# Subtracting the row maximum of the scores in PSUM by matmuls, and another order for the last tiles' routing

## The chip, the cores and the metric

The kernel runs on one core of a Trainium2 chip. The metric is the time of one execution on the device in microseconds (us); the kernel before took 1230.69 us, the median of 3 runs (1223.26 to 1238.8). The engines are TensorE (PE; its weight loads are PEld), VectorE (DVE), ScalarE (ACT), GpSimd (POOL) and SyncE (SP), which only issues transfers here. Each runs its own list of instructions in order, and they wait for one another through semaphores.

## The reference

The layer is a gated cross attention followed by a gated mixture of experts, 32 batches of 256 rows, 256 wide; the context has 77 rows a batch, 16 heads of width 16.

```python
x = x + tanh(g_xattn) * xattn(layernorm(x), ctx, ctx, mask, Wq, bq, Wk, bk, Wv, bv, Wfc, bfc)
x = x + tanh(g_ffn) * ffn(layernorm(x), gate_kernel, w0, w1, wo)

# xattn
energy = einsum('bhqd,bhkd->bhqk', Q, K) / 4
energy = where(mask == 0, -1e10, energy)
attention = softmax(energy, axis=-1)
x = einsum('bhqk,bhkd->bhqd', attention, V) @ Wfc.T + bfc      # heads merged

# ffn: 8 experts, each row goes to the 2 with the largest gate logits
top_k_weights, top_k_indices = top_k(x @ gate_kernel, 2)
weights = softmax(top_k_weights)
output = sum over the 2 experts of weight * ((silu(x @ w0[e]) * (x @ w1[e])) @ wo[e])
```

## The kernel before, in words

The 8192 rows are 64 tiles of 128 query rows, two tiles to a batch. The first part goes through the 32 batches: layer norm, projections, attention, residual, second layer norm, gate, choice of two experts, and a scatter of each row (256 values, its number and its weight) to a buffer in device memory, `routed_rows`, sorted by expert. The second part goes through 135 tiles of that buffer, one expert a tile, and adds the result to the output by an indirect transfer. Between them, DVE computes tables that say which tile belongs to which expert. Expert weights are split in a high and a low part during the first part, stored as `split_weights`, and fetched again.

Every engine has its own hand-written list: one function `batch(b, u, n)` per engine, called for batches 0 to 3 and 30, 31 as straight code and in a loop for the others. The order of the calls there is the order of the work. In it `i` is the batch's first tile, and the work for several tiles is in flight: while tile `i` attends, the scores of `i + 1` are in PSUM, and the gate and routing of tiles `i - 1` to `i - 4` are under way.

The path of a tile's scores: PE writes the mask and the scores of all 16 heads (4 heads in each of 4 PSUM banks, 308 columns in each, 1232 in all) into `psS`, which is single-buffered (`scores`, L1454 and L1460). DVE takes the maximum of each head (`s_largest`, L1075), then subtracts it and writes the result to `prob` in SBUF (`s_shift`, L1079). ACT takes the exponential in place (`exp_scores`, L711). PE transposes `prob` in three groups through `psT` (`prob_T`, L1475), ACT copies each to `probT` (L707), and PE multiplies with the values and a column of ones (`attend`, L1489, 32-column tiles). DVE normalises (L1087, L1090), PE transposes and projects (`o_T` L1499, `project` L1507), DVE adds the residual (L1100). The second norm's output is transposed by `n2_T` (L1517), the gate is L1525, the ranks within an expert are L1530 and L1531. The low part of the next batch's queries is `q_low` (L1033), awaited by the value projection (L1433).

At the end of the first part each engine has straight code for the last tiles. DVE's `route` chooses experts and places rows; POOL numbers rows, computes weights (`weigh`) and scatters (L568, two transfers a tile); SP stores the last split weight piece (`store_piece`, L418), the last output tile (L431), and writes padding rows at the ends of the experts' regions (`pad_experts`, L378), ACT pads the other half. POOL loads the first routed rows (L620) only when the tables, all output tiles, all pads and all scatters are done.

Of the kernel before, what the change touches and what calls it, by code (L numbers as in the profile page):

```python
# [15 lines left out]
P = 128  # L16
# [6 lines left out]
def flamingo_gated_layer(nc, x, ctx_in, mask, g_xattn, g_ffn, Wq, bq, Wk, bk, Wv, bv, Wfc, bfc,  # L23
# [57 lines left out]
    with ExitStack() as ctx, ExitStack() as attention:  # L81
# [85 lines left out]
        mx = sb("mx", [P, 2, H])  # L167
# [68 lines left out]
        psY = psG[:, D:2 * D]  # L236
        assert H * VW + DC * K2 <= 512 and E == 8
# [19 lines left out]

        s_ps, s_max, s_sub, p_done = sem("s_ps"), sem("s_max"), sem("s_sub"), sem("p_done")
# [127 lines left out]
        def _(sp):  # L386
# [69 lines left out]
            batches(sp, batch)  # L456
            store_piece(NQ - 1)
            store_x1(NT - 1, 1)

            pad_experts(sp, range(0, E, 2))  # L460
# [28 lines left out]
        def _(gp):  # L489
# [114 lines left out]
            rstd_2(NT - 1)  # L604
            for i in range(NT - 4, NT):
                number_rows(i, i % 4)
            weigh(B - 2, 0)
            scatter(NT - 4, 0, B - 2)
            scatter(NT - 3, 1, B - 2)
            weigh(B - 1, 1)  # L610
# [50 lines left out]
        def _(act):  # L661
# [47 lines left out]
            def exp_scores(i, t):  # L709
                act.wait_ge(s_sub, i + 1)  # L710
                act.activation(prob[:, t, 0:HK], prob[:, t, 0:HK], ACT.Exp, scale=scale).then_inc(p_done, 1)  # L711
# [152 lines left out]
            o_evac(NT - 1)  # L864
            norm_2(NT - 2, 0, 2, LOOPS - 1)
            n2_evac(NT - 2)
            exp_gap(NT - 3, 1, B - 2)
            gated_evac(NT - 2)
            copy_row(NT - 2, 2)
            norm_2(NT - 1, 1, 3, LOOPS - 1)  # L870
            n2_evac(NT - 1)
# [88 lines left out]
        def _(dve):  # L960
# [34 lines left out]
            dve.memset(prob[:, :, HK:CH * P], 0.0).then_inc(valid_done, 1)  # L995
            dve.wait_ge(valid_done, 17)
# [3 lines left out]
            dve.tensor_copy(pick_key[:].rearrange("p (o k) -> p o k", o=3), ident[0:K2, 0:K2].rearrange("p (o k) -> p o k", o=1).to_broadcast([K2, 3, K2])).then_inc(valid_done, 1)  # L1000
            dve.wait_ge(mask_in[0], 16)
# [71 lines left out]
            def s_largest(i, t):  # L1073
                dve.wait_ge(s_ps, RG * (i + 1))
                dve.tensor_reduce(mx[:, t].rearrange("p (n h) -> p n h", n=RG), S_ALL, AX_X, ALU.max).then_inc(s_max, 1)  # L1075

            def s_shift(i, t):
                dve.wait_ge(s_max, i + 1)
                dve.tensor_tensor(prob[:, t, 0:HK].rearrange("p (n h k) -> p n h k", n=RG, k=K2), S_ALL,  # L1079
                                  mx[:, t].rearrange("p (n h o) -> p n h o", n=RG, o=1).to_broadcast([P, RG, HB, K2]),  # L1080
                                  ALU.subtract).then_inc(s_sub, 1)
# [84 lines left out]
            s_shift(0, 0)  # L1166
# [4 lines left out]
            def batch(b, u, n):  # L1171
# [22 lines left out]
                s_shift(i + 1, 1)  # L1194
# [45 lines left out]
                if more:  # L1240
                    s_shift(i + 2, 0)
# [29 lines left out]
            stats_2(NT - 2, 0, 1)  # L1271
            residual_1(NT - 1, 1, 1, B - 1)
            for part in range(2):
                stats_2(NT - 1, 1, part)
            for i in range(NT - 3, NT):
                route(i)
# [106 lines left out]
        def _(pe):  # L1383
# [62 lines left out]
            def scores(i, u, t, b):  # L1446
# [3 lines left out]
                if known(i, 1):  # L1450
                    pe.wait_ge(s_sub, i)
# [4 lines left out]
                for q_part, k_part in PARTS:  # L1456
                    for c in range(DC):
                        for j in range(RG):
# [43 lines left out]
            def project(i):  # L1502
                pe.wait_ge(oT_sb, DC * (i + 1))
                if known(i, 1):
                    pe.wait_ge(n2T_sb, i)
# [4 lines left out]
            def n2_T(i, u4):  # L1510
                pe.wait_ge(xn2_done, i + 1)
                if below(i, NT - 1):
# [36 lines left out]
            flatten_values(0)  # L1549
            ctx_T(1, 1, 0)  # L1550
            pe.wait_ge(gate_in, 16)
            keys(1)
            x_T(1)
# [3 lines left out]
            def batch(b, u, n):  # L1557
# [39 lines left out]
                if known(i + 1, 2):  # L1597
                    n2_T(i - 1, (u4 - 1) % 4)
                attend(i + 1, u, b, 1)
                attend(i + 1, u, b, 2)  # L1600
# [168 lines left out]
```

## Time and profile before

| what | value |
|---|---|
| median of 3 runs | 1230.69 us (1223.26 to 1238.8) |
| the profiled execution | 1230.18 us |
| its span, first to last instruction | 1228.6 us |
| mean granted TensorE clock | 0.962 of full |
| PE busy, of the span | 1123.8 us (91%) |
| DVE busy | 956.0 us (78%) |
| ACT busy | 702.7 us (57%) |
| POOL busy | 729.3 us (59%) |
| chain that ended last: PE, DVE, issue, DMA | 78%, 8%, 6%, 4% |
| maxima of the scores (L1075), 64 times | 91.8 us busy, 1435 ns each |
| subtraction (L1079), 64 times | 91.5 us busy, 1430 ns each |

The first part ends at about 560 us of the span, the second begins at about 586 us. The shares are averages over both parts, so what the change touches must be read inside the first part and at the passage between them.

### The profile page before, as it was taken

The numbers are of one execution on the slowest core, as the hardware profiler recorded it, in microseconds if no ns is written. First come the engines' busy times: TensorE is split into PE (matmuls) and PEld (weight loads), VectorE is DVE, ScalarE is ACT, GpSimd is POOL, SyncE is SP. The second block draws the span as 40 slices with busy tenths as digits, with TensorE's granted clock in tenths as the row PEclk, the third lists the DMA queues.
The fourth block names the chain that finished last, engine by engine and source line by source line (L and its number), as shares of the span: only waits on it lengthen the run. The fifth ranks groups of instructions, "written<-read, shape, count | busy, mean of one in ns | idle before, by whom it ended". The sixth has DMA issues, their size and how long they took to land.

```text
span 1228.6 us, 46148 instructions
## 1 busy us (share of the span) xinstructions
PE 1123.8 (91%) x14850; PEld 922.4 (75%) x14851; DVE 956.0 (78%) x2702; ACT 702.7 (57%) x1652; POOL 729.3 (59%) x1134
## 2 busy tenths in 40 slices
PE   3999999999999999960899999999879999999994
PEld 2787888888888888740788888888758888888883
DVE  4798999999999999845344688888668888888882
ACT  2787888888888888840343344444334444444441
POOL 3367888888888888744244455555435555555552
PEclk9999999999999999975899999999989999999997
DMA  5144444444444444464688576767888666666672
GB/s 163 34 136 150 152 151 151 151 150 146 144 148 146 146 146 151 142 222 151 197 227 215 114 124 119 120 119 119 156 126 129 120 120 120 119 121 120 120 117 26
DMA packets 193909, 169.74 MB, mean 138 GB/s; under 512 B 130996, under 2 KB 174548, under 8 KB 191668
## 3 DMA queue, kind: packets, MB, share of 16 engines
q1 hardware_dynamic: 158592, 112.54, 34.4%
q0 software_dynamic: 32064, 52.46, 22.3%
q10 hardware_dynamic: 3188, 3.89, 1.4%
q8 instruction: 38, 0.62, 0.2%
q14 instruction: 27, 0.22, 0.1%
HBM read 68.95 MB, written 70.27 MB: 113 GB/s over the span
## 4 chain that ended last, share of the span: by engine, by line
PE 78%; DVE 8%; issue 6%; DMA 4%; ACT 1%; POOL 1%; ACTq 1%; DVEq 0%; POOLq 0%; SPq 0%
PE banks L1658 29%; PE psB L1679 9%; PE psB L1489 5%; PE psT L1475 5%; PE psB L1682 5%; PE psG L1507 5%; PE psA L1426 3%; PE banks L1460 3%; PE psA L1433 3%; PE psG L1637 2%; DMA hT<-hs 2%; PE psA L1443 2%; DVE mx L1075 2%; PE psG L1499 2%; DVE prob L1079 1%
## 5 line engine op out<-in xcount | busy, mean ns | idle before, releaser
L1658 PE MATMUL banks<-w_all,etT 128*128 x1620 | 431.5, 403 | 12.6 <-DVE etT L1345 11.5
L633 POOL DMA_INDIRECT out_dram<-ey,eid x135 | 216.7, 1605 | 218.1 <-PE psG L1637 106.8
L1658 PEld LDWEIGHTS banks<-w_all,etT 128*128 128x128 f32 x1620 | 288.1, 190 | 62.3 <-DVE etT L1345 12.4
L909 ACT ACTIVATE ey<-psB,ewt 128x256 f32<-128x256 f32 x135 | 64.2, 476 | 191.0 <-PE psB L1682 190.8
L620 POOL DMA_DIRECT2D et<-routed_rows x135 | 101.3, 750 | 115.1 <-issue 114.9
L568 POOL DMA_INDIRECT routed_rows<-rows,slot x128 | 126.5, 988 | 44.9 <-issue 33.5
L1679 PE MATMUL psB<-w_all,hgT 128*128 x540 | 147.2, 394 | 4.7 <-DVE ey L1355 3.9
L881 ACT CAST etT<-psG 128x256 fp32r<-128x256 f32 x135 | 50.6, 375 | 151.6 <-PE psG L1637 148.9
L707 ACT COPY probT<-psT 128x512 f32<-128x512 f32 (+1 forms) x192 | 98.9, 515 | 48.9 <-PE psT L1475 46.5
L1679 PEld LDWEIGHTS psB<-w_all,hgT 128*128 128x128 f32 x540 | 100.8, 189 | 29.2 <-issue 5.9
L1475 PE MATMUL psT<-ident,prob 128*128 128x128 f32 x640 | 104.9, 279 | 7.0 <-ACT gated L733 4.2
L1355 DVE SCALAR_TENSOR_TENSOR ey<-psB,ewt,ey 128x256 f32<-128x256 f32 x135 | 65.2, 483 | 50.5 <-ACT ey L909 49.9
L890 ACT ACTIVATE hs<-banks 128x512 f32<-128x512 f32 x135 | 80.9, 600 | 35.8 <-PE psT L1668 32.5
L1341 DVE COPY hT<-hT 128x1024 uint16<-128x1024 uint16 x113 | 84.5, 748 | 18.2 <-DMA hT<-hs 16.9
L1345 DVE TENSOR_TENSOR etT<-psG,etT 128x256 fp32r<-128x256 f32 x135 | 57.1, 423 | 49.3 <-ACT etT L881 48.6
L1075 DVE TENSOR_REDUCE mx<-banks 128x16 f32<-128x1232 f32 x64 | 91.8, 1435 | 3.0 <-PE banks L1460 3.0
L1322 DVE TENSOR_TENSOR hs<-banks,hs 128x512 f32<-128x512 f32 x135 | 92.3, 683 | 1.8 <-PE banks L1658 1.8
L1682 PEld LDWEIGHTS psB<-w_all,hgT 128*128 128x128 f32 x540 | 83.3, 191 | 11.4
L1079 DVE TENSOR_TENSOR prob<-banks,mx 128x1232 f32<-128x1232 f32 x64 | 91.5, 1430 | 0.1
L1475 PEld LDWEIGHTS psT<-ident,prob 128*128 128x128 f32 x640 | 75.7, 143 | 20.4 <-issue 9.4
L1334 DVE COPY hs<-hs 128x1024 uint16<-128x1024 uint16 x113 | 79.4, 702 | 12.4
L1489 PE MATMUL psB<-vbd,probT 128*32 128x51 f32 x5120 | 87.6, 212 | 0.0
(177 smaller groups left out, 2335.2 us busy)
## 6 DMA issues: line engine op xcount, KB each, us to landing
split_weights<-w_part SPq DMA_DIRECT2D x16, 1536.0 KB, 6.2
w_all<-split_weights SPq DMA_DIRECT2D x28, 768.0 KB, 4.5
et<-routed_rows POOLq DMA_DIRECT2D x135, 129.0 KB
xb<-in_x_dram SPq DMA_DIRECT2D x32, 256.0 KB, 3.1
w_raw<-in_L_ffn_w_kernel_dram SPq DMA_DIRECT2D x32, 256.0 KB
out_dram<-x SPq DMA_DIRECT2D x64, 128.0 KB
w_raw<-in_L_ffn_wo_kernel_dram SPq DMA_DIRECT2D x16, 256.0 KB
cb<-in_ctx_dram SPq DMA_DIRECT2D x32, 77.0 KB
```

The lines of the kernel that those rows point to most:

```text
L568: gp.indirect_dma_start(out=routed, out_offset=bass.IndirectOffsetOnAxis(ap=slot[:, u4, k:k + 1], axis=0), in_=rows[:, u4, k, :], in_offse ...
L620: gp.dma_start(et[:, u % 2], routed[bass.ds(r * P, P), :]).then_inc(et_in[u % 2], 16)
L633: gp.indirect_dma_start(out=out, out_offset=bass.IndirectOffsetOnAxis(ap=eid[:, u % 8:u % 8 + 1], axis=0), in_=ey[:, u % 4, :], in_offset= ...
L707: act.copy(probT[:, c0:c1].rearrange("p c q -> p (c q)"), psT[:, 0:(c1 - c0) * P]).then_inc(t_sb, 1)
L1075: dve.tensor_reduce(mx[:, t].rearrange("p (n h) -> p n h", n=RG), S_ALL, AX_X, ALU.max).then_inc(s_max, 1)
L1079: dve.tensor_tensor(prob[:, t, 0:HK].rearrange("p (n h k) -> p n h k", n=RG, k=K2), S_ALL, mx[:, t].rearrange("p (n h o) -> p n h o", n=RG ...
L1322: dve.tensor_tensor(hs[:], banks4[:, 2 + u % 2], hs[:], ALU.mult).then_inc(hg_done, 1)
L1475: m = pe.transpose(psT[:, (c - c0) * P:(c - c0 + 1) * P], prob[:, t, c * P:(c + 1) * P], ident[:])
L1489: m = pe.matmul(psB[r0:r0 + ROWS, h * VW:(h + 3) * VW], probT[:, c, r0:r0 + ROWS], vbd[:, u, c].rearrange("p h d -> p (h d)"), start=(c == ...
L1658: m = pe.matmul(banks4[:, bank], etT[:, u % 2, a, c], weight(e, c, w, n), start=(j == 0), stop=(j == len(steps) - 1))
L1679: pe.matmul(psB[:, 0:2 * D], hgT[:, u % 2, 0, c], weight_pair(e, c), start=(c == 0), stop=False, skip_group_check=True)
L1682: m = pe.matmul(psB[:, 0:D], hgT[:, u % 2, 1, c], weight(e, c // 2, 0, 2, c % 2 * D, D), start=False, stop=(c == FC - 1), skip_group_check ...
```

## The change

In the attention, DVE still takes the maximum of each head, but writes the 16 values of a query row to 16 of 128 columns of a tile `mx`, four at the head of each group of 32 columns. PE multiplies this tile with the identity, which gives its transpose in unused columns of the first score bank (`max_T`). DVE copies the transpose to SBUF (`max_evac`), and PE multiplies it with a constant matrix that has -1 where a head's row meets its 77 columns, accumulating into the scores in PSUM (`shift`, four matmuls of 32 rows, one for each bank). ACT's exponential reads the four banks and writes `prob`. The whole-tile subtraction on DVE is gone; the next tile's scores wait for the exponential instead of the subtraction.

At the end of the first part: PE projects the last tile before it transposes the second-last tile's norm; DVE routes tile NT-3 before the last residual; ACT and POOL take some steps in another order, POOL scatters two tiles before it numbers the last two; SP writes its pads before it stores the last weight piece.

```diff
@@ -164,7 +164,9 @@
-        mx = sb("mx", [P, 2, H])
+        mx = sb("mx", [P, P])
+        mxT = sb("mxT", [P, P], F32R)
+        minus_head = sb("minus_head", [P, HB, K2], F32R)
...
+        psM = psS[:, 0, HB * K2:HB * K2 + P]
@@ -454,10 +458,9 @@
             batches(sp, batch)
+            store_x1(NT - 1, 1)
+            pad_experts(sp, range(0, E, 2))
             store_piece(NQ - 1)
-            store_x1(NT - 1, 1)
-
-            pad_experts(sp, range(0, E, 2))
@@ -601,12 +604,14 @@
             rstd_2(NT - 2)
-            rstd_2(NT - 1)
-            for i in range(NT - 4, NT):
+            for i in range(NT - 4, NT - 2):
                 number_rows(i, i % 4)
             weigh(B - 2, 0)
+            rstd_2(NT - 1)
             scatter(NT - 4, 0, B - 2)
             scatter(NT - 3, 1, B - 2)
+            for i in range(NT - 2, NT):
+                number_rows(i, i % 4)
             weigh(B - 1, 1)
@@ -707,8 +712,10 @@
             def exp_scores(i, t):
-                act.wait_ge(s_sub, i + 1)
-                act.activation(prob[:, t, 0:HK], prob[:, t, 0:HK], ACT.Exp, scale=scale).then_inc(p_done, 1)
+                act.wait_ge(s_sub, RG * (i + 1))
+                if known(i, 2):
+                    act.wait_ge(t_ps, 3 * (i - 1))
+                act.activation(prob[:, t, 0:HK].rearrange("p (n q) -> p n q", n=RG), psS[:, 0:RG, 0:HB * K2], ACT.Exp, scale=scale).then_inc(p_done, 1)
...
             o_evac(NT - 1)
+            exp_gap(NT - 3, 1, B - 2)
             norm_2(NT - 2, 0, 2, LOOPS - 1)
             n2_evac(NT - 2)
-            exp_gap(NT - 3, 1, B - 2)
-            gated_evac(NT - 2)
             copy_row(NT - 2, 2)
             norm_2(NT - 1, 1, 3, LOOPS - 1)
+            gated_evac(NT - 2)
             n2_evac(NT - 1)
@@ -993,11 +1000,17 @@
+            for j in range(RG):
+                r0 = j * ROWS
+                dve.tensor_scalar(minus_head[r0:r0 + ROWS], ident[r0:r0 + ROWS, r0:r0 + HB].rearrange("p (h o) -> p h o", o=1).to_broadcast([ROWS, HB, K2]),
+                                  -1.0, None, ALU.mult).then_inc(head_rows, 1)
...
             def s_largest(i, t):
                 dve.wait_ge(s_ps, RG * (i + 1))
-                dve.tensor_reduce(mx[:, t].rearrange("p (n h) -> p n h", n=RG), S_ALL, AX_X, ALU.max).then_inc(s_max, 1)
-
-            def s_shift(i, t):
-                dve.wait_ge(s_max, i + 1)
-                dve.tensor_tensor(prob[:, t, 0:HK].rearrange("p (n h k) -> p n h k", n=RG, k=K2), S_ALL,
-                                  mx[:, t].rearrange("p (n h o) -> p n h o", n=RG, o=1).to_broadcast([P, RG, HB, K2]),
-                                  ALU.subtract).then_inc(s_sub, 1)
+                if known(i, 1):
+                    dve.wait_ge(mT_ps, i)
+                dve.tensor_reduce(mx[:].rearrange("p (n s) -> p n s", n=RG)[:, :, 0:HB], S_ALL, AX_X, ALU.max).then_inc(s_max, 1)
+
+            def max_evac(i):
+                dve.wait_ge(mT_ps, i + 1)
+                if known(i, 1):
+                    dve.wait_ge(s_sub, RG * i)
+                dve.tensor_copy(mxT[:], psM).then_inc(mT_sb, 1)
...
             stats_2(NT - 2, 0, 1)
+            route(NT - 3)
             residual_1(NT - 1, 1, 1, B - 1)
             for part in range(2):
                 stats_2(NT - 1, 1, part)
-            for i in range(NT - 3, NT):
-                route(i)
+            route(NT - 2)
+            route(NT - 1)
@@ -1448,7 +1464,7 @@
                 if known(i, 1):
-                    pe.wait_ge(s_sub, i)
+                    pe.wait_ge(p_done, i)
...
+            def max_T(i):
+                pe.wait_ge(s_max, i + 1)
+                pe.matmul(psM, mx[:], ident[:], start=False, stop=True, skip_group_check=True).then_inc(mT_ps, 1)
+
+            def shift(i):
+
+                pe.wait_ge(mT_sb, i + 1)
+                for j in range(RG):
+                    r0 = j * ROWS
+                    pe.matmul(psS[:, j, 0:HB * K2], mxT[r0:r0 + ROWS], minus_head[r0:r0 + ROWS].rearrange("p h k -> p (h k)"),
+                              start=False, stop=True, skip_group_check=True).then_inc(s_sub, 1)
...
                 attend(i, u, b, 0)
+                max_T(i + 1)
                 if known(i, 2):
                     n2_T(i - 2, (u4 - 2) % 4)
                 attend(i, u, b, 1)
                 attend(i, u, b, 2)
+                shift(i + 1)
                 if known(i, 1):
                     project(i - 1)
...
             o_T(NT - 1)
+            project(NT - 1)
             n2_T(NT - 2, 2)
-            project(NT - 1)
```

In the calls of DVE's list `s_shift(i, t)` is replaced by `max_evac(i)` at the same place. The orders of instructions below show where this puts the new ones. A name such as `banks<-ident,mx` gives the tile written and those read; `banks` is the score banks, `psT`, `psB`, `psG` and `psA` are the other PSUM tiles.

PE, second half of a batch in the loop, before:

```order
L1489 MATMUL psB<-vbd,probT 32x51 x16
L1438 REGISTER_ALU
L1443 MATMUL psA<-vparts,pick_key 128x48 x30
L1471 REGISTER_ALU
L1475 MATMUL psT<-ident,prob 128x128 x2
L1513 REGISTER_ALU
L1517 MATMUL psG<-ident,rows 128x128 x2
L1489 MATMUL psB<-vbd,probT 32x51 x16
L1480 REGISTER_ALU
L1489 MATMUL psB<-vbd,probT 32x51 x8
L1507 MATMUL psG<-wfcT,onT 128x256 x2
```

and in the changed kernel:

```order
L1545 MATMUL psG<-ident,rows 128x128 x2
L1483 REGISTER_ALU
L1484 MATMUL banks<-ident,mx 128x128
L1517 MATMUL psB<-vbd,probT 32x51 x16
L1508 REGISTER_ALU
L1517 MATMUL psB<-vbd,probT 32x51 x8
L1491 MATMUL banks<-minus_head,mxT 128x308 x4
L1535 MATMUL psG<-wfcT,onT 128x256 x2
```

The maximum's matmul stands between the transposes of the norm (now L1545) and the rest of attending (now L1517), the four shifts between attending and the projection (now L1535).

SP, from the pads to the fetches of the expert weights, in the changed kernel (before, the store of `split_weights` and a store of `out_dram` stood ahead of the pads):

```order
L381 TENSOR_LOAD base_i
L381 ISA x2
L382 ISA
L382 DMA routed_rows<-pad_rows 128x258
L422 DMA split_weights<-w_part 128x3072
L428 DMA w_all<-split_weights 128x1536 x20
```

The rows shown are the last of four pads, the store of the last piece and what follows.

POOL, the last tiles, in the changed kernel:

```order
L554 COPY rows<-token_id 128x2 x2
L560 TENSOR_SCALAR wsum<-egap 128x2
L562 TENSOR_TENSOR wrec<-wsum,neg_one 128x2
L564 TENSOR_TENSOR rows<-wrec,tanhg 128x2
L566 TENSOR_TENSOR rows<-rows,egap 128x2
L543 TENSOR_SCALAR ve<-mv 128x1
L544 TENSOR_SCALAR neg<-mv 128x1
L548 TENSOR_TENSOR rs<-ve,half_neg 128x1
L550 TENSOR_TENSOR shift<-neg,rs 128x1
L571 DMA routed_rows<-rows,slot 67456x258 x4
L554 COPY rows<-token_id 128x2 x2
```

Before, both norms (the rows from `ve` to `shift`) and four copies of row numbers stood ahead of the first weights. Now the weights of tiles 60 and 61 come ahead of the last tile's norm, and their four scatters ahead of the last two tiles' numbers.

## Rows read from the trace of the kernel before

**Rows 1.** Stretches: us, busy time per engine (instructions), granted clock, DMA share, GB/s

```profile
77.50:470.00 392.50, 385.04 (x9111) 315.57 (x9109) 363.94 (x1237) 343.78 (x856) 314.81 (x657) 1.00 0.44 145
```

**Rows 2.** Order of time, PE: start, duration, what, idle before

```profile
118.36 0.81 PE L1426 MATMUL psA<-xnT,wqT 128*128 128x256 f32 x3
...
306.53 1.89 PE L1426 MATMUL psA<-xnT,wqT 128*128 128x256 f32 x8
...
319.50 0.63 PE L1475 MATMUL psT<-ident,prob 128*128 128x128 f32 x4 [0.23 <-ACT gated L733]
...
322.09 1.89 PE L1426 MATMUL psA<-xnT,wqT 128*128 128x256 f32 x8
...
494.69 0.38 PE L1426 MATMUL psA<-xnT,wqT 128*128 128x256 f32 x1
```

**Rows 3.** Waits of PE's weight loads, 77.5 to 505 us: total, times, longest

```profile
PEld psA L1433 <- DVE qT L1033: 1.9, 11, 0.2
```

**Rows 4.** The chain that ended last, in order of time: start, duration, what

```profile
309.14 0.37 PE psG L1517 x2
309.51 0.69 PE psB L1489 x48
...
313.18 0.24 PE banks L1454 x4
...
314.42 0.44 PE psT L1475 x4
...
316.48 0.22 PE psG L1517 x2
...
317.38 1.07 PE psG L1507 x4
318.64 0.48 DVE x L1100
```

**Rows 5.** Groups by line and form, 200 to 472 us: busy us, mean ns, idle before

```profile
L1079 DVE TENSOR_TENSOR prob<-banks,mx 128x1232 f32<-128x1232 f32 x35 | 50.0, 1429 | 0.0
L711 ACT ACTIVATE prob<-prob 128x1232 f32<-128x1232 f32 x35 | 43.2, 1234 | 0.0
L707 ACT COPY probT<-psT 128x512 f32<-128x512 f32 x70 | 41.1, 587 | 9.5 <-PE psT L1475 8.0
...
L1046 DVE SCALAR_TENSOR_TENSOR kT<-psB,bias,valid 128x77 f32<-128x77 f32 x34 | 8.6, 294 | 1.7 <-issue 1.2
```

**Rows 6.** Order of time, 540 to 586 us; the last row is from the page's DMA issues

```profile
548.22 2.05 PE L1507 MATMUL psG<-wfcT,onT 128*128 128x256 f32 x4 [0.55 <-ACT xn2T L721]
550.31 0.48 DVE L1100 SCALAR_TENSOR_TENSOR x<-psG,tanhg,xg 128x256 f32<-128x256 f32 x1 [6.80 <-PE psG L1507]
557.08 1.05 POOL L568 DMA_INDIRECT routed_rows<-rows,slot  x1 [0.82 <-POOL rows L563]
568.44 0.23 DVE L1307 CAST tblk_i<-tblk 128x135 int32<-128x135 f32 x1
569.32 0.96 POOL L568 DMA_INDIRECT routed_rows<-rows,slot  x1 [0.30 <-issue]
570.31 2.49 POOL L574 TENSOR_TENSOR w_part<-w_raw,w_part 128x512 fp32r<-128x512 f32 x2
572.82 0.34 SPq L418 DMA_DIRECT2D split_weights<-w_part  x1
575.24 4.59 SPq L378 DMA_DIRECT2D routed_rows<-pad_rows  x4
583.18 0.61 POOL L620 DMA_DIRECT2D et<-routed_rows  x1 [10.38 <-issue]
585.67 0.66 PE L1637 MATMUL psG<-ident,et 128*128 128x128 f32 x2 [26.69 <-DMA et<-routed_rows]
...
split_weights<-w_part SPq DMA_DIRECT2D x16, 1536.0 KB, 6.2
```

**Rows 7.** Order of time, PE, at the start of the kernel

```profile
30.90 1.25 PE L1409 MATMUL psB<-ctxT,wkT 128*32 128x77 f32 x32 [2.89 <-ACT ctxT L684]
```

More of the change, by code:

```diff
@@ L256, in flamingo_gated_layer @@
         v_nat, v_part, v_rest = sem("v_nat"), sem("v_part"), sem("v_rest")
+        mT_ps, mT_sb, head_rows = sem("mT_ps"), sem("mT_sb"), sem("head_rows")
         s_ps, s_max, s_sub, p_done = sem("s_ps"), sem("s_max"), sem("s_sub"), sem("p_done")
@@ L456, in _ @@
             batches(sp, batch)
-            store_piece(NQ - 1)
             store_x1(NT - 1, 1)
             pad_experts(sp, range(0, E, 2))
+            store_piece(NQ - 1)
             sp.wait_ge(pad_out, 16 * (1 + E + SPARE))
@@ L995, in _ @@
             dve.memset(prob[:, :, HK:CH * P], 0.0).then_inc(valid_done, 1)
+            dve.memset(mx[:], 0.0).then_inc(head_rows, 1)
             dve.wait_ge(valid_done, 17)
@@ L1000, in _ @@
             dve.tensor_copy(pick_key[:].rearrange("p (o k) -> p o k", o=3), ident[0:K2, 0:K2].rearrange("p (o k) -> p o k", o=1).to_broadcast([K2, 3, K2])).then_inc(valid_done, 1)
+            for j in range(RG):
+                r0 = j * ROWS
+                dve.tensor_scalar(minus_head[r0:r0 + ROWS], ident[r0:r0 + ROWS, r0:r0 + HB].rearrange("p (h o) -> p h o", o=1).to_broadcast([ROWS, HB, K2]),
+                                  -1.0, None, ALU.mult).then_inc(head_rows, 1)
+            dve.wait_ge(head_rows, 1 + RG)
             dve.wait_ge(mask_in[0], 16)
@@ L1165, in _ @@
             s_largest(0, 0)
-            s_shift(0, 0)
+            max_evac(0)
             v_evac(0, 0)
@@ L1193, in batch @@
                     k_low(b + 1)
-                s_shift(i + 1, 1)
+                max_evac(i + 1)
                 if known(i, 3):
@@ L1240, in batch @@
                 if more:
-                    s_shift(i + 2, 0)
+                    max_evac(i + 2)
                 o_norm(i + 1, 0)
@@ L1504, in project @@
                 if known(i, 1):
-                    pe.wait_ge(n2T_sb, i)
+                    pe.wait_ge(n2T_sb, i if below(i, NT - 1) else i - 1)
                 for c in range(DC):
@@ L1511, in n2_T @@
                 pe.wait_ge(xn2_done, i + 1)
-                if below(i, NT - 1):
+                if below(i, NT - 2):
                     pe.wait_ge(oT_sb, DC * (i + 2))
@@ L1549, in _ @@
             flatten_values(0)
+            max_T(0)
             ctx_T(1, 1, 0)
@@ L1552, in _ @@
             keys(1)
+            shift(0)
             x_T(1)
@@ L1598, in batch @@
                     n2_T(i - 1, (u4 - 1) % 4)
+                if more:
+                    max_T(i + 2)
                 attend(i + 1, u, b, 1)
                 attend(i + 1, u, b, 2)
+                if more:
+                    shift(i + 2)
                 if known(i + 1, 1):
```

## The prediction

> **What bounds the kernel now.** I read the stretches first, then the tensor engine's order of time, then the chain of waits, and last the single durations. One stretch covers the steady attention loop: there the matmul row of TensorE (PE below) is busy for 385.04 of 392.5 us, VectorE (DVE) for 363.94, ScalarE (ACT) for 343.78, at full granted clock [rows 1]. The reader should see two engines near full, so the next question is which one sets the pace. The start of the query projection marks a batch (two tiles of 128 query rows). From 306.53 to 322.09 a batch takes 15.56 us; from 118.36 to 494.69 there are 24, 15.68 us each on average, so that the other of each pair takes about 15.80 [rows 2]. PE has one visible stall in the 15.56 us batch, 0.23 us before the transposes of the probabilities, which wait for ACT [rows 2]; the longer batch has 0.2 us more, before the value projection, waiting for DVE's low part of the queries [rows 3]. Without stalls PE needs 15.56 - 0.23 = 15.33 us. So PE is the bound, and at most 15.68 - 15.33 = 0.35 us a batch can come back by relieving DVE.
>
> At the junction between attention and experts PE stands still for 26.69 us until the first routed rows are there [rows 6].
>
> **DVE, per tile.** Removed: the subtraction over 1232 columns, 1.43 us. Added: a copy of 128 PSUM columns. Two rows bracket it, 0.29 us for 77 columns and 0.48 us for 256; by their slope (0.19/179 per column) 128 columns are an estimated 0.34 us [rows 5, 6]. DVE loses 1.09 us of work a tile, 2.2 a batch. But it isn't the bound. It must also wait inside its queue: the new copy stands where the subtraction was and waits for the transposed maximum, which PE issues only after the first part of attending. Behind it stand the low part of the queries, the normalisation and the residual. In the batch that begins at 306.53 PE reached that place 2.6 us later, at 309.14 [rows 4]. With the added matmul and 0.34 us of copy DVE goes on at about 310.0, some 1 us later than now; the queries' low part is then ready at about 311.8, and PE, itself later by both new groups, asks for it at about 312.1. I cost this wait at nothing; its cover is the 0.3 us just named.
>
> **ACT, per tile.** The exponential takes 1.23 us from SBUF. From PSUM, ACT copied 512 columns in 0.59 us, so 1232 columns are at most 1.41 us by that rate, and 1.23 if the source doesn't matter [rows 5]. I take 1.23: ACT has 1.9 us a batch free. Its chain (PE's shift, the exponential, the gate's copy, then the next transposes) takes some 1.7 us, while PE has the output projection (1.1), gate, rank and keys or values to do in between, about 2.0 to 2.3. So the exponential's new place in the chain costs nothing, and the 0.23 us stall goes, since PE comes 0.5 us later. The scores' new wait for the exponential costs nothing either: in PE's order the transposes of the same tile's probabilities stand ahead of it and need the same event.
>
> **PE, per tile: the term that counts.** Added: one fp32 matmul of the maximum with the identity, 128 columns, and four row-tiled matmuls of 308 columns. The trace has no such fp32 matmul. The nearest rows are the transposes, four of 128 columns in 0.44 us. A full fp32 matmul appears as two records, so twice 0.11 = 0.22 us. The upper bound is a pair of transposes right behind column-tiled work, 0.37 [rows 4]. In the first half of a batch the new one stands ahead of just such a pair and takes over its change of mode, in the second behind one. So I take 0.25. For the four shifts the nearest row is the mask's group, also four matmuls of 308 columns: 0.24 us, a change of mode included [rows 4]. It is bf16 where the shift is a 32-bit type, so I take 0.28, with 0.24 and 0.40 as ends. Sum 0.53 us a tile, from 0.46 to 0.77.
>
> A rule speaks against the change here. Attending with 32-column tiles and then projecting at full width already costs a change of mode (a pair takes 0.37 us behind attending and 0.22 behind a transpose, 0.15 between them [rows 4]); the shift puts a third mode in between. The Trainium skill, "TensorEngine Tiling (Array Packing)", Key Properties, says that a change of tiling mode drains the engine. Both agree. If the mask's 0.24 did not contain that drain, a tile would cost 0.15 more and the sum below 9.3 us more.
>
> 62 tiles lie in the stretch that PE bounds: 62 x 0.53 = +32.9 us. Recovered: 0.35 us a batch for 29 batches, -10.2 us. Net +22.7. A new batch is then 15.33 + 1.06 = 16.4 us.
>
> **The start.** The builds of the -1 matrix (four of 308 columns) go into DVE's idle time before the first weights: free. For the first tile PE does the maximum ahead of the second context's transposes and keys. Those keys ran at 30.90 us, before the first maximum was ready [rows 7]; they now come about 1.3 us later, and the first exponential with them. Against that, DVE's chain gets shorter over the next two tiles. I take +1, with -2 and +3 as ends.
>
> **The junction.** Three edits, read from the same rows [rows 6]:
> 1. Projection of the last tile ahead of the second-last tile's normalised transposes. It started at 548.22 though its own input was there at about 544.3: PE stood before the transposes ahead of it, for ACT. It now starts at about 544.4; the last residual, DVE at 550.31, comes about 4 us sooner, and with it the last routing and the tables, finished at 568.7 and now at about 564.6.
> 2. Scatters. GpSimd (POOL) issued all eight from 557.08 to 570.28, about 1.3 us each. Four can now go at about 550 to 555, the other four when the last slots are ready, 558 to 563.3. Then the two low parts (2.49 us): POOL is free at about 565.8 instead of 572.8.
> 3. SyncE's queue. The pads were issued from 575.24 to 579.83, behind the store of the last weight piece, which waited for POOL until 572.82. Only then, at 583.18, were the first routed rows asked for. The pads' own condition was met at 560. Ahead of the store they end by about 562.5, and no longer count.
> So the load of the first rows is issued at about 566 instead of 583.18: 17 us. Late next is the store: its 1.5 MB takes 6.2 us and now runs beside that load, which took 2.4 us alone. If the load lands with the store, 4 us are lost. I take -15.5, ends -17 and -11.
>
> **Sum.** The profiled execution took 1230.18 us (span 1228.6), 0.5 us under the median of the runs, 1230.69. 1230.2 + 22.7 + 1 - 15.5 = 1238.4. Forecast **1238 us**: slower by 0.6%, which is no difference at the 2% (24.6 us) that I take as the least a measurement of this kernel can tell, its runs lying 1223 to 1239.
>
> **Rivals.**
> - *Tight waits and changes of mode (slower).* A tile costs PE the upper 0.77 us, and in the second half of each batch only part of attending (0.69 us) covers the way from the maximum over DVE's copy to the shift: a handoff to DVE of 0.2 (PE's projection ends at 318.45, DVE begins at 318.64 [rows 4]), the copy 0.34 and a handoff back of the same 0.2 fill it entirely. If they exceed it by 0.3, 31 batches cost 9 us more. 1230.2 + 47.7 + 9 - 10.2 + 1 - 15.5 = 1262. It is over 2% from 0.8 us a tile in all. For it: each handoff has a cost that PE can't hide. Against it: the only groups with such shapes take 0.22 to 0.37 and 0.24. Chance 0.13.
> - *The junction gives little.* The store delays the load of rows, or the scatters still end last because the weights of the last pair wait for the last gap: -5 instead of -15.5, 1249. For it: the store's transfer and the rows' use the same 16 engines. Chance 0.15.
> - *The new matmuls hide (faster).* Were DVE the true bound, PE's added work would fall into its slack: 1230.2 - 10.2 + 1 - 15.5 = 1205.5. Against it: PE's pieces stand end to end in the chain in both halves. Chance 0.05.
> - *DVE becomes later.* The wait for the maximum holds up the queries' low part by more than the 0.3 us of cover, and the 0.35 us a batch are not recovered: 1238.4 + 10.2 = 1249. Chance 0.12.
> - Forecast as worked out: 0.55.
>
> **Range.** The ends of the forecast's own terms are 1238.4 - 4.3 (0.46 a tile) - 1.5 - 3 = 1230 and, with one upper end, 1253. Reaching halfway to the faster rival and over both rivals at 1249 gives **1219 to 1256**. Slower by over 2% (above 1254.8): the first rival and a tail of others, 0.16. Faster by over 2% (below 1206): 0.05. Within: 0.79.
>
> **What would show it.** In the new profile: batches of 16.4 us between query projections; the new matmul of the maximum at about 0.25 us and the group of four at about 0.28 in the chain; no stall of PE for the gate's copy or the queries' low part; DVE idle around 1 us a batch ahead of the new copy; the first load of routed rows issued about 17 us sooner after the end of attention. The prediction is wrong if the batch is at or below 15.7 us (the matmuls hide), above 16.8 (waits or mode changes), or if pads, scatters or the store still stand in the chain before that load.

## The result, and the profile after

The changed kernel takes 1244.28 us (median of 9 runs, 1241.91 to 1250.84), the kernel before 1229.32 in the runs beside it (9 runs, 1222.44 to 1240.23): ratio 1.0118, 95% interval 1.0079 to 1.0158. It is 1.2% slower, in the range of 1219 to 1256; the forecast was 1238. The effect itself was about twice the forecast one: 15.0 us between the medians, where 0.6% (7.7 us) was forecast.

From the page of the changed kernel: the busy time of its engines, and the share of each in the chain of work that ended last.

```profile
PE 1155.6 (93%) x15234; PEld 946.7 (76%) x15235; DVE 890.1 (72%) x2707; ACT 712.7 (57%) x1652; POOL 728.9 (59%) x1134
...
PE 91%; DMA 3%; issue 2%; DVE 2%; ACT 1%; POOL 1%; ACTq 1%; POOLq 0%; SPq 0%; DVEq 0%
```

DVE lost 66 us of work and its share of the chain fell from 8% to 2%. PE gained 32 us of busy time, and the kernel got longer with PE and not shorter with DVE. The steady loop shows it better. The stretch of [rows 1] in the changed kernel (busy time per engine in the same order):

```profile
77.50:470.00 392.50, 390.43 (x8926) 318.23 (x8925) 296.13 (x1177) 332.96 (x810) 297.67 (x621) 1.00 0.42 138
```

PE is busy for 99.5% of it, DVE for 75% (before 98% and 93%). The starts of the query projection, as in [rows 2], in the order of time of PE:

```profile
56.08 0.38 PE L1442 MATMUL psA<-xnT,wqT 128*128 128x256 f32 x1
...
308.29 0.38 PE L1442 MATMUL psA<-xnT,wqT 128*128 128x256 f32 x1
...
324.88 0.38 PE L1442 MATMUL psA<-xnT,wqT 128*128 128x256 f32 x1
...
540.61 0.38 PE L1442 MATMUL psA<-xnT,wqT 128*128 128x256 f32 x1
```

Every steady batch takes 16.59 us, where they alternated between 15.56 and 15.8: +0.91 on the average of 15.68. The new groups stand in the chain, first half of a batch and then second half:

```profile
310.91 0.42 PE banks L1484 x2
311.32 0.22 PE psG L1545 x2
311.54 0.69 PE psB L1517 x48
312.23 0.34 PE banks L1491 x3
312.57 1.06 PE psG L1535 x4
...
318.81 0.22 PE psG L1545 x2
319.03 0.22 PE banks L1484 x2
319.25 0.69 PE psB L1517 x48
319.94 0.34 PE banks L1491 x3
```

The maximum's matmul takes 0.42 us behind attending, but relieves the transposes after it of 0.15 (0.22 us, and 0.37 in [rows 4]), net 0.27; behind transposes it takes 0.22. The four shifts take 0.34. The other pieces keep their length to within 0.06 us, except the transposes of x, which take 0.60 in this chain and 0.44 in that of E5, where they come up again. DVE waits for the maximum, PE does not wait for DVE's copy (waits from 77.5 to 505 us, total, times, longest):

```profile
DVE mxT L1096 <- PE banks L1484: 53.6, 51, 1.9
```

The junction in the order of time, the rows that answer to [rows 6]; SPq is SyncE's queue of transfers:

```profile
580.61 5.87 SPq L428 DMA_DIRECT2D w_all<-split_weights  x2
586.52 0.45 SPq L435 DMA_DIRECT2D out_dram<-x  x1
588.51 4.37 SPq L382 DMA_DIRECT2D routed_rows<-pad_rows  x4
593.61 0.34 SPq L422 DMA_DIRECT2D split_weights<-w_part  x1
...
591.10 2.48 POOL L577 TENSOR_TENSOR w_part<-w_raw,w_part 128x512 fp32r<-128x512 f32 x2
599.05 0.61 POOL L625 DMA_DIRECT2D et<-routed_rows  x1 [5.46 <-issue]
```

From these marks the 14.1 us between the two spans divide as follows. The marks of before are 52.01 and 510.25 for the second and the last query projection, and 583.18 for the first load of routed rows [rows 6].

| stretch | before | after | difference | forecast |
|---|---|---|---|---|
| start to the second query projection | 52.0 | 56.1 | +4.1 | +1 |
| to the last one, 30 batches | 458.2 | 484.5 | +26.3 | +22.7 (whole stretch) |
| to the first load of routed rows (junction) | 72.9 | 58.4 | -14.5 | -15.5 |
| to the end of the span | 645.4 | 643.7 | -1.8 | 0 |

One batch of the 30 is not steady, the one in which the straight code gives way to the loop: 19.57 us before and 20.43 in the changed kernel. In the changed kernel PE stops in it for 2.07 us, without a wait that the profile shows, and then runs at the lower of its two clocks (granted clock 0.50, which is 1.2 GHz) for some 3 us. Order of time, and the stretch from 120 to 123 us in the columns of [rows 1]:

```profile
119.38 0.47 PE L1491 MATMUL banks<-minus_head,mxT 32*128 32x308 f32 x3 [2.07 <-issue]
119.77 2.07 PE L1535 MATMUL psG<-wfcT,onT 128*128 128x256 f32 x4
```

```profile
120.00:123.00 3.00, 3.00 (x54) 2.43 (x54) 0.95 (x2) 1.83 (x4) 0.60 (x1) 0.50 0.23 80
```

The projection of four matmuls takes 2.07 us there and 1.13 in the steady loop. The kernel before has the same thing (a stop of 2.60 us, granted clock 0.50 from 112 to 115), so it cancels between these two. Between the kernels below it does not.

### The profile page after: what moved, and what is told of

Its sections match the earlier page's. It is cut to its first block, busy times and chain, and to the rows that moved or that the text cites. A ratio compares the mean times of both kernels' runs of the same rounds, so it can differ in the third digit from the quotient of the medians.

```text
span 1242.7 us, 47084 instructions
## 1 busy us (share of the span) xinstructions
PE 1155.6 (93%) x15234; PEld 946.7 (76%) x15235; DVE 890.1 (72%) x2707; ACT 712.7 (57%) x1652; POOL 728.9 (59%) x1134
## 4 chain that ended last, share of the span: by engine, by line
PE 91%; DMA 3%; issue 2%; DVE 2%; ACT 1%; POOL 1%; ACTq 1%; POOLq 0%; SPq 0%; DVEq 0%
PE banks L1694 30%; PE psB L1715 10%; PE psT L1503 6%; PE psB L1517 6%; PE psG L1535 5%; PE psB L1718 5%; PE psA L1442 5%; PE banks L1476 3%; PE psG L1673 2%; PE psA L1449 2%; PE psA L1459 2%; PE psG L1527 2%; PE banks L1491 2%; PE banks L1484 2%; PE psB L1425 2%
## 5 line engine op out<-in xcount | busy, mean ns | idle before, releaser
L1715 PE MATMUL psB<-w_all,hgT 128*128 x540 | 147.1, 394 | 4.8 <-DVE ey L1371 3.9
L1517 PE MATMUL psB<-vbd,probT 128*32 128x51 f32 x5120 | 85.5, 211 | 2.0 <-issue 2.0
L1718 PE MATMUL psB<-w_all,hgT 128*128 x540 | 85.8, 282 | 0.0
```

The lines of the kernel that those rows point to most:

```text
L1517: m = pe.matmul(psB[r0:r0 + ROWS, h * VW:(h + 3) * VW], probT[:, c, r0:r0 + ROWS], vbd[:, u, c].rearrange("p h d -> p (h d)"), start=(c == ...
L1715: pe.matmul(psB[:, 0:2 * D], hgT[:, u % 2, 0, c], weight_pair(e, c), start=(c == 0), stop=False, skip_group_check=True)
L1718: m = pe.matmul(psB[:, 0:D], hgT[:, u % 2, 1, c], weight(e, c // 2, 0, 2, c % 2 * D, D), start=False, stop=(c == FC - 1), skip_group_check ...
```

## The experiments

Each kernel's median stands beside the kernel before on the same chip, as a ratio. Stage times are from each kernel's profiled execution. Steady batches repeat to 0.02 us. The stretches before and after them, and the batch at the entry of the loop, differ by some us even between kernels that share PE's order, so they count for less.

**E1 and E2: the two halves of the change by themselves.** E1 keeps the attention part and undoes the end; E2 keeps the end and lets DVE subtract.

Three of the end's edits, E1 against the changed kernel:

```diff
+            store_piece(NQ - 1)
             store_x1(NT - 1, 1)
...
-            store_piece(NQ - 1)
...
-            route(NT - 3)
...
-            route(NT - 2)
-            route(NT - 1)
+            for i in range(NT - 3, NT):
+                route(i)
...
+            n2_T(NT - 2, 2)
             project(NT - 1)
-            n2_T(NT - 2, 2)
```

E2 makes the opposite edits to the kernel before, and so keeps DVE's subtraction.

> The change's attention part alone; the end of the first part is in the old order. Theory A (PE's own added work sets the batch, the new order of the end is a separate gain): batches of 16.59 us as in the changed kernel, the first routed rows asked for about 73 us after the last query projection as before the change, total about 1229 + 0.91 x 29 + 4 = 1260 us. Rival (the parts lean on one another, the end gains only because DVE is freed): the end is short here too, total about 1245.

> The kernel before with the new order of the end alone. Theory A: batches 15.56 and 15.8 us, the first routed rows asked for about 58 us after the last query projection, total about 1229 - 16 = 1213 us. Rival: the end stays near 73 us because DVE still subtracts there, total 1225 to 1229.

E1 took 1255.99 us, ratio 1.0238 (1.0168 to 1.0307); E2 took 1213.07 us, ratio 0.9861 (0.98 to 0.9921). Batches of 16.59 us in E1; 15.55 and 15.8 in E2. E1, the last query projection and the first load of rows:

```profile
536.82 0.38 PE L1440 MATMUL psA<-xnT,wqT 128*128 128x256 f32 x1
...
610.10 0.61 POOL L624 DMA_DIRECT2D et<-routed_rows  x1 [10.55 <-issue]
```

E2, the same two marks:

```profile
507.82 0.38 PE L1428 MATMUL psA<-xnT,wqT 128*128 128x256 f32 x1
...
567.24 0.61 POOL L621 DMA_DIRECT2D et<-routed_rows  x1 [8.19 <-issue]
```

That is 73.3 us in E1 (old end, DVE relieved) and 59.4 in E2 (new end, DVE subtracting), against 72.9 and 58.4 in the kernels before and after. The gain at the end does not need the relieved DVE. The change is two changes of opposite sign: the attention part costs 2.4%, the end gives 1.4%.

**E3: no maximum and no shift.** It leaves out the maximum, its transpose, the copy and the shift, and gives masked keys -60 instead of -1e10.

```diff
-MASKED = -1e10
+MASKED = -60.0
...
-                max_T(i + 1)
...
-                shift(i + 1)
...
-                act.wait_ge(s_sub, RG * (i + 1))
+                act.wait_ge(s_ps, RG * (i + 1))
```

> The changed kernel without the maximum, its transpose and the shift: the exponential reads the scores as they are, and masked keys get -60 where they had -1e10. Theory A: PE's batch falls by its two groups, 2 x (0.22 + 0.34) and what they cost their neighbours, to 15.4 to 15.5 us, total about 1207. Rival (another engine would be the bound at once, for instance DVE's residual and value copies ahead of PE's transposes of x): 15.7 or more, total 1215 or more.

1207.19 us, ratio 0.9807 (0.974 to 0.9873); batch 15.53 us:

```profile
252.85 0.60 PE L1434 MATMUL psA<-xnT,wqT 128*128 128x256 f32 x2
...
268.39 0.60 PE L1434 MATMUL psA<-xnT,wqT 128*128 128x256 f32 x2
```

Here DVE does neither maximum nor subtraction, 2.86 us a tile less than before, and PE does exactly the work of before. The forecast's bound was 0.35 us back by relieving DVE, a batch of 15.33. E3 gained 0.15 on 15.68. PE's stall for ACT's copy of the gate is still there, though no maximum is waited for:

```profile
250.27 0.63 PE L1495 MATMUL psT<-ident,prob 128*128 128x128 f32 x4 [0.20 <-ACT gated L740]
```

So that stall was not DVE's. It lies in ACT's queue, where two activations of the next norm (1.1 us) stand ahead of the exponential and the copy, without a gap (order of time):

```profile
247.84 1.10 ACT L696 ACTIVATE xn<-xb,shift,rs 128x256 f32<-128x256 f32 x2
248.84 1.19 ACT L718 ACTIVATE prob<-banks 128x1232 f32<-128x1232 f32 x1
249.92 0.18 ACT L740 COPY gated<-psT 128x24 f32<-128x24 f32 x1
```

**E4: the same operations in bf16.** Waits and order are those of the changed kernel. The subtracted value needs no precision, since the same rounded maximum leaves all keys of a head and cancels in the softmax.

```diff
-        mx = sb("mx", [P, P])
-        mxT = sb("mxT", [P, P], F32R)
-        minus_head = sb("minus_head", [P, HB, K2], F32R)
+        mx = sb("mx", [P, P], BF16)
+        mxT = sb("mxT", [P, P], BF16)
+        ident16 = sb("ident16", [P, P], BF16)
+        minus_head = sb("minus_head", [P, HB, K2], BF16)
...
-                pe.matmul(psM, mx[:], ident[:],
+                pe.matmul(psM, mx[:], ident16[:],
```

> The changed kernel with the maximum, its transpose and the -1 matrix in bf16; all waits, handoffs and the instruction order stay. Theory A (work sets the batch): the maximum's matmul falls from 0.22 to about 0.08 us, the shift from 0.34 to between 0.24 (like the mask's group) and 0.34; batch 16.1 to 16.35 us, total about 1232 to 1239. Rival (handoffs from PE over DVE back to PE set it): batch 16.5 to 16.6, total 1243. If the shift stays at 0.34, its excess over the mask's group is the change of tiling mode, not the type.

1223.67 us, ratio 0.9971 (0.9945 to 0.9997). Batch 15.97 us, 0.62 less. In the chain, the second half of one batch and the first half of the next:

```profile
257.36 0.06 PE banks L1486
257.41 0.69 PE psB L1519 x48
258.10 0.24 PE banks L1493 x4
...
265.56 0.16 PE banks L1486
265.73 0.23 PE psG L1547 x2
265.95 0.69 PE psB L1519 x48
266.64 0.24 PE banks L1493 x4
```

The maximum falls from 0.42 and 0.22 to 0.16 and 0.06 us, the shift from 0.34 to 0.24: 0.26 + 0.16 + 2 x 0.10 = 0.62, all of the batch's gain. Theory A holds: every handoff stayed as it was, and the batch fell by the work alone. The maximum's matmul in bf16 was expected at 0.08 us. It took that or less behind transposes and twice that behind attending, but the net saving was larger than expected, so the batch (16.1 to 16.35 expected) and the total (1232 to 1239 expected) both came out below their bounds. E4 also settles why the shift was longer than the mask's group: it was the 32-bit type. In bf16 it equals the mask's 0.24 [rows 4], in spite of its place between 32-column tiles and full width. With the new end, however, even the bf16 form (0.9971 of the kernel before) is slower than DVE's subtraction (E2, 0.9861).

**E5: what PE waits for before the transposes of x, and the start.** In the changed kernel the gate's stall was gone, but the weight load for the transposes of x came 0.18 us late; DVE's copy of the values ends just ahead of it, at 306.00 (order of time):

```profile
304.95 0.48 DVE L1115 SCALAR_TENSOR_TENSOR x<-psG,tanhg,xg 128x256 f32<-128x256 f32 x1 [0.69 <-PE psG L1535]
305.35 0.65 DVE L1078 TENSOR_TENSOR vbd<-psA,head_of 128x480 f32<-128x480 f32 x1
306.12 0.42 PEld L1435 LDWEIGHTS psA<-ident,xn 128*128 128x128 f32 x4 [0.18 <-issue]
```

```diff
+                if more:
+                    v_evac(b + 1, 1 - u)
                 if known(i + 1, 1):
                     residual_1(i, u, 0, b)
-                if more:
-                    v_evac(b + 1, 1 - u)
...
+            ctx_T(1, 1, 0)
             max_T(0)
-            ctx_T(1, 1, 0)
+            shift(0)
             pe.wait_ge(gate_in, 16)
             keys(1)
-            shift(0)
             x_T(1)
```

> The changed kernel with two orders altered: DVE copies the next batch's values ahead of the residual, and at the start PE does the second context's transposes ahead of the first maximum, and the first shift ahead of the keys. Theory A (the 0.18 us that PE waits before the transposes of x comes from DVE's copy of the values standing behind the residual): that wait goes and the batch is 16.4 us; at the start the delay of 4 us against the kernel before falls to 2 to 3. Total about 1237 us. Rival (the transposes of x wait for something else, as ACT's norm): batch 16.59, total 1242.

1239.71 us, ratio 1.0108 (1.0073 to 1.0144). The batch is 16.42 us (252.07 to 268.49), and the second query projection starts at 52.54 instead of 56.08:

```profile
52.54 0.38 PE L1442 MATMUL psA<-xnT,wqT 128*128 128x256 f32 x1
...
252.07 0.60 PE L1442 MATMUL psA<-xnT,wqT 128*128 128x256 f32 x2
...
268.49 0.38 PE L1442 MATMUL psA<-xnT,wqT 128*128 128x256 f32 x1
```

The wait was DVE's residual ahead of the values' copy: 0.17 us a batch. E5 also corrects the base of the forecast. Less the new groups (0.49 + 0.68) its batch is 15.25 and not 15.33, so 0.08 more comes back than the 0.23 of the stall's row. The projection behind the shift is a part of that: 1.06 us in the first half of a batch, and 1.10 in E3 without the shift.

The start's order is worth some 2 to 3 us: four kernels with the changed order reach this mark at 54.7 to 56.1 us, four with the altered one at 51.3 to 53.7. The five kernels with DVE's subtraction reach it at 52.0 to 55.1. Kernels of one order thus differ by up to 3 us, and the size is uncertain. The total of 1239.7 lies between the two expectations, 1237 and 1242; the batch decides for the first.

**E6: what still ends last at the junction.** SyncE fetches weight pieces 2 and 3 behind the pads instead of in the last batch.

```diff
+                fetch = early and u == 0
-                if early:
+                if fetch:
...
-            for q in range(EARLY, RING):
+            for q in range(DC, RING):
```

> The changed kernel with the fetches of weight pieces 2 and 3 moved on SyncE from the last batch to behind the pads. Theory A (after the change the pads still end last at the junction, because SyncE's queue holds the fetches): the first routed rows are asked for about 53 us after the last query projection instead of 58.4, total about 1239. Rival (the scatters or the tables end last anyway): 57 to 58 us, total 1244.

1255.22 us, ratio 1.0224 (1.0165 to 1.0282): a miss in the total, though the junction did what was expected. The marks are 539.81 and:

```profile
594.32 0.61 POOL L626 DMA_DIRECT2D et<-routed_rows  x1 [1.76 <-issue]
```

54.5 us, 3.9 less. Without the fetches the pads go out at 582.66, 42.9 us after the last query projection instead of 47.9. But four more transfers (4.3 to 6.7 us each) now stand on SyncE's queue ahead of the first transposes of the expert part, which the queue issues at tile 20. The end of the fetches on SyncE, and PE's first long stall in the expert part:

```profile
702.50 11.71 SPq L428 DMA_DIRECT2D w_all<-split_weights  x3
714.35 13.56 SPq L483 DMA_TRANSPOSE hT<-hs  x4
...
720.75 1.22 PE L1695 MATMUL banks<-w_all,etT 128*128 x2 [10.50 <-DVE etT L1362]
```

In the changed kernel the queue is free at 691.8, 92.7 us after the first load of rows, and no stall stands at this place; here it is 120 us after it. From the first load to the end E6 takes 658.1 us, 14.4 more than the changed kernel, and this stall is 10.5 of them. The 3.9 us won at the junction do not cover it.

**E7 and E8: the end of E6 with DVE's subtraction, and with bf16.** Both also copy the values ahead of the residual; E8 has the altered start of E5 as well, which is not shown. The lines stand against E2 for E7, and against E4 for E8.

```diff
-                if early:
+                fetch = early and u == 0
+                if fetch:
...
-            for q in range(EARLY, RING):
+            for q in range(DC, RING):
...
+                if more:
+                    v_evac(b + 1, 1 - u)
                 if known(i + 1, 1):
                     residual_1(i, u, 0, b)
-                if more:
-                    v_evac(b + 1, 1 - u)
```

> The kernel before (DVE subtracts) with the new order of the end, the values copied ahead of the residual, and the fetches behind the pads. Theory A: batches as before the change or 0.05 us shorter, the end 5 us shorter than in the kernel with the new end alone, total about 1207 us.

> The maximum by matmuls in bf16 with the values' copy ahead, the altered start and the fetches behind the pads. Theory A: batch 15.97 - 0.18 = 15.8 us, junction about 53 us, total about 1223.7 - 5 - 2 - 5 = 1212 us. Rival: one of the three doesn't add up with the others, 1218 or more.

E7: 1220.46 us, ratio 0.9964 (0.9931 to 0.9998). E8: 1225.94 us, ratio 0.9995 (0.9968 to 1.0022). The batches are as expected (15.54 and 15.83; 15.80), so the values' copy gives E7 nothing, where PE doesn't wait for it. The junctions take 52.4 and 56.6 us. Both miss their totals by 13 to 14 us (1207 and 1212 were expected). PE's stall at the first transposes, with the queue free 115 and 114 us after the first load, is a part of it: 4.59 us in E7 and 7.25 in E8. In E7's profiled execution (1215.77, its fastest run) the stretch after the first load is 7.8 us longer than E2's, which takes back the 7.0 gained at the junction; why the median lies 4.7 above that run is open. E8's junction stayed 3.6 us over the 53 that were expected, and its last stretch is 11.9 longer than E4's, more than the stall. I estimated from the 10.5 us at 120 that the queue may be busy until about 109 us without a stall; E7 and E8 give 110 and 107 in the same way.

**E9, E10, E12: only piece 3 behind the pads**, two transfers instead of four: DVE's subtraction without the values' order (E9), bf16 (E10) and fp32 (E12) with all the orders above.

```diff
-            for q in range(EARLY, RING):
+            for q in range(EARLY - 1, RING):
```

> The kernel before with the new order of the end, and only weight piece 3 (two transfers) moved behind the pads. Theory A (in e6 the junction got shorter, but four more transfers on SyncE's queue held up the first transposes of the expert part; the queue may end up to about 109 us after the first rows are asked for): junction 53 to 54.5 us, queue ends at about 107 us, no stall of PE over 2 us near tile 22, total about 1213 - 4 = 1209 us. Rival (the stall comes from something else that moving any fetch causes): a stall of some us stays, total 1213 or more.

> The maximum by matmuls in bf16, the values' copy ahead, the altered start, and only weight piece 3 behind the pads. Theory A: as e8 without its 7 us stall, total about 1217 us. Rival: 1224 or more.

> The changed kernel with the values' copy ahead, the altered start and only weight piece 3 behind the pads; the maximum stays fp32. Theory A: batch 16.42 us, junction about 55 us, total about 1239.7 - 4 = 1235 us, so 18 us more than the same kernel in bf16 (30 batches of 0.62).

| kernel | median us | ratio (95%) | batch | junction |
|---|---|---|---|---|
| E9 | 1216.83 | 0.9904 (0.9875 to 0.9932) | 15.55, 15.8 | 54.3 |
| E10 | 1215.36 | 0.9899 (0.9857 to 0.994) | 15.80 | 55.7 |
| E12 | 1238.15 | 1.008 (1.004 to 1.012) | 16.43 | 57.4 |

The stall at the first transposes is gone in all three; in E9 the queue is free 105 us after the first load. E10 (1217 expected) is 22.8 us faster than E12 (1235 expected), of which 30 x 0.62 = 18.6 are the type. E9 was expected at 1209 and is no faster than E2. Its profiled execution reached the second query projection 2.1 us later than E2's (55.14 against 53.08), its batch at the entry of the loop took 20.29 us where E2's took 15.86, and its last stretch was 2.7 us longer, against 5.1 gained at the junction. E2 and E9 differ in SyncE's list alone. In E9 PE stopped for 3.32 us in the entry batch and ran at a granted clock of 0.50 from 117 to 119 us, and E2 shows neither. Each has one profiled execution, so whether such a step belongs to the kernel or to the run isn't shown, and whether E9's shorter junction is worth anything stays open. The best kernel with matmuls (E10, 0.9899) is no faster than the two with DVE's subtraction (E2 0.9861, E9 0.9904), so no run here shows a gain from moving the subtraction.

**E11: the 0.23 us stall, by ACT's order.** E2 with the exponential ahead of the next norm.

```diff
-                if more2:
-                    norm_1(b + 2, u)
                 if more:
                     exp_scores(i + 2, 0)
+                if more2:
+                    norm_1(b + 2, u)
```

> The kernel before with the new order of the end, and in the second half of a batch ACT takes the exponential ahead of the next norm. It tests the 0.35 us a batch that were forecast to come back. If PE's 0.23 us stall is only ACT's order, the batches fall to 15.35 and 15.6 us, total about 1206. If the transposes of x, which need that norm and DVE's copy of the values, take over the wait, the batches stay at 15.5 to 15.8, total 1211 to 1213.

1235.83 us, ratio 1.0072 (1.0045 to 1.0099), 22.8 us more than E2: neither expectation. Batch 16.38 us. ACT in the order of time:

```profile
265.92 1.23 ACT L712 ACTIVATE prob<-prob 128x1232 f32<-128x1232 f32 x1 [0.75 <-DVE prob L1080]
267.06 1.08 ACT L692 ACTIVATE xn<-xb,shift,rs 128x256 f32<-128x256 f32 x2
268.04 0.15 ACT L734 COPY gated<-psT 128x24 f32<-128x24 f32 x1
```

The exponential now waits for DVE's subtraction with the norm behind it, and the norm delays the gate's copy, for which PE waited 15.7 us in 17 waits between 200 and 472 us. The old order filled that wait with the norm. So the old order of ACT made the 0.23 us stall, but this new one costs more than it.

## Why the prediction was right or wrong, point by point

- *PE is the bound, and the added matmuls cost their full time:* right. E1 alone lengthens the batch to 16.59, E3 takes the groups out and comes to 15.53, E4 shortens them by 0.62 and the batch by 0.62. That DVE is not the bound: right, it lost 66 us of work and the kernel got slower. Its copy took 0.29 us, where 0.34 was estimated.
- *The maximum's matmul, 0.25 us:* 0.27 and 0.22. Right.
- *The four shifts, 0.28 us (0.24 to 0.40):* 0.34. Too small by 0.06 a tile, 3.7 us over 62 tiles. I took the bf16 row and added a little for the type; E4 shows that the type is the whole difference of 0.10.
- *The 0.35 us a batch that come back:* too large, since it left out the next wait. The stall for ACT went as forecast, since PE comes later, and it gave even more than its row showed (15.25 as the base in E5, not 15.33). But a wait of 0.17 us came up in its place before the transposes of x, behind DVE's residual (E5). So 15.68 + 1.17 - 16.59 = 0.26 us came back and not 0.35. The forecast of 16.39 and the measured 16.59 differ by 0.20: the dearer groups +0.11, the new wait +0.17, the lower base -0.08. Taken as what relieving DVE gives, the bound of 0.35 holds but is far from reached: E3 relieves DVE of both passes and gains 0.15.
- *The waits in DVE's and ACT's queues cost nothing:* right. DVE stood 53.6 us in its queue for the maximum, about 2 us a batch where 1 was forecast, and the queries' low part, for which PE's weight loads had waited [rows 3], no longer holds PE. The exponential takes 1.19 us from PSUM, 1.23 from SBUF.
- *The third tiling mode:* the weighed rule would have added 9.3 us. A change of mode shows (the maximum costs 0.20 us more behind attending than behind transposes, in bf16 0.10), but the bf16 shift equals the mask's group, so that no cost of a change of mode beyond the mask's row appears. The nearest row was the right price, but for the type.
- *The start, +1 us:* +4.1 in the two profiled executions, above the upper end of +3. The mechanism was the named one, keys held up behind the first maximum (they ran at 33.33 instead of 30.90, 2.4 us later where 1.3 was forecast), and E5's order takes it away. A part of the 4 us is spread: the kernels with DVE's subtraction reach the mark between 52.0 and 55.1, the kernel before at the low end.
- *The junction, -15.5 us:* -14.5. The size is right, but partly by luck, and one of the prediction's own signs of being wrong came true: the pads still ended last before the load. They were forecast to end at about 562.5 on the old marks. Their own condition, the final positions, was indeed met early (DVE's L1306 ended at 582.71, 42.1 us after the last query projection, where the kernel before took 49.9). But they were issued at 588.51, because SyncE's fetches of weights, each waiting for the one before, held the queue until 586.48. POOL was free at 593.58 and the load went out at 599.05. Without the fetches (E6) the load goes 3.9 us sooner. Two misses offset this. POOL was free 53.0 us after the last query projection, where the forecast's own marks give 55.6 (565.8 less 510.25). And 1.5 us were set aside for the store delaying the first load, which did not happen: the load took 2.4 us as before.
- *The rivals:* tight handoffs did not show (E4). "The new matmuls hide" is refuted. "The junction gives little" did not happen, though what it names (something still ends last) did. "DVE becomes later" came true in small, with 0.17 us a batch behind the copy of the values and not behind the queries' low part. The likeliest case was the right one, short by 6 us: 3.6 in the 30 batches, 3.1 at the start, 1.0 at the junction, less 1.8 behind it.

The last stretch, -1.8 us, is not explained. Its length lay between 641.5 (E1) and 648.7 us (E9) in all kernels without the stall of E6, and the edits touch the lists there only by two fetches on SyncE (E9, E10, E12). A good part of this spread is one stall of PE some 310 us after the first load, 7.67 us in E1 and 11.93 in E9; between the kernels before and after it differs by only 0.3 (10.09 and 9.79).

## What to carry to other kernels

Work that was moved to the engine that bounds the loop cost its full time there, however idle the relieved engine became. Price such work by the nearest group of the same shape and the same type, and where the value need not be precise (a maximum that cancels in the softmax), use the narrow type. Before counting a stall as won, find the order that makes it. Here it lay in ACT's queue, relieving DVE brought back little, and the next wait (0.17 us) stood close behind. A transfer that is moved to the back of a queue delays what the queue issues later; in E6 the stall came some 120 us after the point that the edit shortened.

## What the runs showed of the hardware

- Four row-tiled matmuls (32 rows each) of 308 columns took 0.34 us with fp32r operands and 0.24 with bf16, at the full granted clock in both; a matmul of 128 columns against the identity took 0.22 us in fp32 (two records) and 0.06 in bf16 (one).
- The batch at the entry of the loop took between 15.6 and 21.4 us in the profiled executions of these 14 kernels, with no wait for another engine that the profile shows. In the five that took over 19 us (before, changed, E6, E9, E11) PE stopped for 2.07 to 3.32 us and then ran at a granted clock of 0.50 for 3 to 7 us. In the other nine the clock stayed at 1.00; of these, E5 and E12 had a stop of 2.02 us and took 18.85. So the same batch can differ by 4 to 5 us between kernels whose steady batches are alike, more than most of the orders tried here. What makes the stop isn't shown.
